# Row tiles 4 to 7 are loaded after ctx parts 12 to 14 have been quantised, instead of among parts 6 to 12

## The chip, the cores and the metric

The kernel runs on one core of a Trainium2 chip. The metric is device microseconds (us) for one execution. The kernel before was timed three times; the median counts. One further execution was profiled, and all rows below come from that one.

## The reference

x has 2 batches of 1024 rows of 2048 columns, ctx has 2 batches of 2048 by 2048. All data is float32.

```python
q1 = fake_quant(layernorm(x), x1_scale, x1_zp)     # clip(round(v/s + z), 0, 255), then (q - z)*s
q2 = fake_quant(ctx, x2_scale, x2_zp)
x  = x + q1 @ q2                                   # 1024x2048 by 2048x2048, per batch
qg, qu = quantised rows of layernorm(x)*inv_gate, layernorm(x)*inv_up
inter  = clip(silu(qg @ w_gate.T * scales) * (qu @ w_up.T * scales), -10, 10)
x  = x + (quantised rows of inter*inv_inter) @ w_down.T * scales
```

Only the first product, for the first batch, has to do with the change.

## The kernel before

**Tiles.** The 2048 rows of x are 16 row tiles of 128 rows (tile m, 1 MB each, `x_tile` in the trace). Tiles 0 to 7 are batch 0. ctx comes in 32 parts of 1 MB (part q, `ctx_stage`); four parts make one chunk of 512 columns, so parts 0 to 15 are batch 0. Stage one has 64 groups of 16 matmuls. Groups 0 to 15 multiply row tiles 0 to 3 with chunks 0 to 3 (group g takes tile g % 4 and chunk g // 4); groups 16 to 31 multiply tiles 4 to 7 with the same four chunks. Group 8 is thus the first to need parts 8 to 11, group 12 the first to need parts 12 to 15, group 16 the first to need tile 4.

**What happens to a ctx part.** A DMA of the ACT queue (L439) brings it into one of three staging buffers. DVE quantises it (L762) to eight bits, or ACT (L446) where q % 4 is 3; ACT (L455) or POOL (L698) casts it to fp16 for TensorE. ACT issues later parts between its casts: the load of part q waits until part q - 3 has been quantised. DVE also adds up the cast parts (`col_add`, L779 and L782) for a column sum, which TensorE multiplies by ones (L1048) after groups 6, 9, 11 and 14.

**What happens to a row tile.** SP issues its load (L259). DVE takes its statistics (L789), POOL makes the scale (L652 to L656), ACT quantises it (`x_i`, L462) and casts it (`x_q`, L470). For tiles 4 and up SP then issues a DMA transpose (`q1T`, L266). There is a single `x_q` buffer: the cast of tile m waits until the transpose of tile m - 1 has landed.

**What sets the order.** Each engine runs a list written out by hand, in step with the groups. On DVE, at group g, the column sums come first, then the quantisation of a part (part 12 at group 8, 13 at 9, 14 at 10), then row statistics (tile 4 at group 10, 5 at 11, 6 at 13, 7 at 14), and last the evacuation of group g (L808), which waits for its matmuls. On SP the list of loads 0 to 7 is followed by the transposes of tiles 4 to 6, the store of x2 tile 0 (L270), the transpose of tile 7, the stores of x2 tiles 1 to 3 and the loads of tiles 8 to 11. Tiles 4 to 7 go to space in SBUF of their own, so that their loads wait for no buffer: the wait on `c_quant` in front of each one only places them in time. `c_quant` counts the parts that DVE has quantised, and `plain(q)` is its count when part q is done.

Of the kernel before, what the change touches and what calls it, by code (L numbers as in the profile page):

```python
# [12 lines left out]
def build(nc, x, ctx_t, params, w_gu, sw_gu, w_dn, sw_dn, inv_gate, inv_up, inv_inter, out):  # L13
# [23 lines left out]
    with ExitStack() as stack:  # L37
# [5 lines left out]
        def sem(name):  # L43
            return stack.enter_context(nc.semaphore(name))
# [84 lines left out]
        c_quant, c_cast = sem("c_quant"), sem("c_cast")  # L129
# [91 lines left out]
        def plain(q):  # L221
            return q + 1 - (q + 1) // 4
# [21 lines left out]
        def _(sp):  # L244
            def load_x(m):
                if 4 <= m < 8:
                    sp.wait_ge(c_quant, plain((6, 8, 10, 12)[m - 4]))
                elif 8 <= m < 12:
                    sp.wait_ge(x2_stored[m % 8], 16)
                elif m == 13:  # L250
                    sp.wait_ge(c3_cast, QUADS // 4)
                elif m in (12, 14):
                    sp.wait_ge(c_quant, plain(30 if m == 12 else 29))
                elif m == 15:
                    sp.wait_ge(x2_stored[0], 32)
                if m == 0:
                    sp.dma_start(X[0][:, 0:D // 2], x_f[0:P, 0:D // 2]).then_inc(x_loaded[0], 16)
                    return
                sp.dma_start(X[m][:, :], x_f[m * P:(m + 1) * P, :]).then_inc(x_loaded[m % 8], 16)  # L259
# [56 lines left out]
            for m in range(8):  # L316
                load_x(m)
# [6 lines left out]
            for m in range(8, 12):  # L324
                load_x(m)
# [4 lines left out]
            for m in range(12, 15):  # L330
                load_x(m)
# [816 lines left out]
```

## Time and profile before

| what | value |
|---|---|
| median of 3 runs | 1054.46 us (1053.47 to 1055.18) |
| the profiled execution: its time, and its span | 1058.52 us, 1056.8 us |
| TensorE (PE) busy in the span | 939.6 us, 89% |
| VectorE (DVE), ScalarE (ACT), GpSimd (POOL) busy | 666.1, 360.4, 295.3 us |
| mean granted TensorE clock | 0.950 of full speed |
| loads of x on SP: count, size, median to landing | 15, 1024 KB, 9.4 us |
| loads of ctx on ACT: count, size, median to landing | 32, 1024 KB, 8.1 us |

The span is the time from the first to the last instruction; the profiled time holds 1.7 us more. A shift of one stage counts only if what follows starts earlier or later by it.

### The profile page before, as it was taken

The page shows a single profiled execution, that of the slowest core. Times are in us where ns is not written, and L with a number is a line of the kernel's source. Part 1 is how long each engine was busy: PE and PEld are TensorE (multiplying, and loading weights), DVE is VectorE, ACT ScalarE, POOL GpSimd, SP SyncE. Part 2 cuts the span into 40 slices and gives each one's busy share as a digit, 9 for nine tenths or more (in the row PEclk, how much of TensorE's full clock was granted, in tenths as well). Part 3 has the DMA queues.
Part 4 walks back from the last instruction along what each step waited for, and adds up shares of the span by engine and source line. Part 5 has one row for each costly group of instructions (what it writes and reads, how often), then busy time and mean ns, then how long its engine had stood idle before and what let it go on. Part 6 is the DMA issues. An engine that isn't in the chain of part 4 may idle for free.

```text
span 1056.8 us, 11253 instructions
## 1 busy us (share of the span) xinstructions
PE 939.6 (89%) x4192; PEld 416.0 (39%) x4192; DVE 666.1 (63%) x1006; ACT 360.4 (34%) x281; POOL 295.3 (28%) x256
## 2 busy tenths in 40 slices
PE   1689886799696778899999999999959989999998
PEld 1333332344242333344444444444424434444443
DVE  5469374657396777666777777777566694444443
ACT  4735456456445652222222333333226520000000
POOL 2226655364356021333333323223420000000000
PEclk9799988899897888899999999999989989999999
DMA  9665797976848803231333333333349630994112
GB/s 356 240 268 199 245 368 227 350 271 204 289 165 274 282 21 78 79 71 54 89 90 90 90 90 90 90 90 90 80 125 336 255 110 1 314 347 136 80 80 79
DMA packets 131686, 179.52 MB, mean 170 GB/s; under 512 B 111024, under 2 KB 111024, under 8 KB 113968
## 3 DMA queue, kind: packets, MB, share of 16 engines
q1 hardware_dynamic: 126848, 144.72, 43.8%
q10 hardware_dynamic: 4752, 34.08, 8.1%
q8 instruction: 33, 0.54, 0.2%
q0 software_dynamic: 32, 0.00, 0.1%
q14 instruction: 21, 0.17, 0.1%
HBM read 113.77 MB, written 37.75 MB: 143 GB/s over the span
## 4 chain that ended last, share of the span: by engine, by line
PE 58%; DVE 12%; issue 10%; DMA 8%; POOL 5%; ACT 5%; ACTq 0%; SPq 0%; DVEq 0%; POOLq 0%
PE ps L1099 36%; PE ps L1111 19%; DVE w_slots L849 5%; POOL x_tile L691 3%; PE ps L1079 3%; DMA ctx_stage<-in_ctx 2%; DVE small_operands L789 2%; DMA q1T<-x_q 2%; ACT x_i L462 1%; DMA w_raw<-in_w_gu 1%; DMA x_tile<-in_x 1%; DMA w_raw<-in_w_dn 1%; DVE ctx_u L762 1%; POOL ctx_slot L698 1%; DMA qT_odd<-q_f 1%
## 5 line engine op out<-in xcount | busy, mean ns | idle before, releaser
L1079 PE MATMUL ps<-ctx_slot,q1T 128*128 128x512 f16 x1024 | 237.2, 394 | 22.5 <-DMA q1T<-x_q 11.1
L1099 PE MATMUL ps<-w_slots,qT_even 128*128 128x512 f16 x1024 | 233.5, 391 | 21.1 <-issue 8.6
L1099 PE MATMUL ps<-w_slots,qT_odd 128*128 128x512 f16 x1024 | 231.9, 389 | 21.8 <-issue 19.7
L1111 PE MATMUL ps<-w_slots,qiT 128*128 128x512 f16 x1024 | 224.1, 382 | 4.1 <-DVE gate_and_up L891 4.1
L1079 PEld LDWEIGHTS ps<-ctx_slot,q1T 128*128 128x128 f16 x1024 | 102.7, 101 | 154.4 <-issue 16.8
L1099 PEld LDWEIGHTS ps<-w_slots,qT_even 128*128 128x128 f16 x1024 | 102.0, 100 | 151.8 <-issue 32.2
L1099 PEld LDWEIGHTS ps<-w_slots,qT_odd 128*128 128x128 f16 x1024 | 101.8, 100 | 151.2 <-issue 35.2
L1111 PEld LDWEIGHTS ps<-w_slots,qiT 128*128 128x128 f16 x1024 | 100.8, 99 | 127.3 <-DVE w_slots L849 4.6
L529 ACT ACTIVATE q_f<-q_i 128x2048 f16<-128x2048 int8 x32 | 61.1, 1910 | 195.0 <-DVE q_i L861 190.1
L920 DVE SCALAR_TENSOR_TENSOR down_tmp<-ps,small_operands,down_scales_b 128x512 f32<-128x512 f32 x64 | 48.0, 750 | 99.3 <-PE ps L1111 99.2
L870 DVE TENSOR_REDUCE small_operands<-x_and_xs 128x1 f32<-128x2048 f32 x19 | 43.4, 2284 | 105.9 <-POOL x_and_xs L672 102.3
L691 POOL TENSOR_TENSOR x_tile<-x_tile,col_bias 128x512 f32<-128x512 f32 x64 | 92.5, 1467 | 39.4 <-DVE x_tile L808 39.4
L808 DVE SCALAR_TENSOR_TENSOR x_tile<-ps,small_operands,x_tile 128x512 f32<-128x512 f32 x64 | 46.6, 734 | 57.1 <-PE ps L1079 56.9
L849 DVE SCALAR_TENSOR_TENSOR w_slots<-w_raw,small_operands,w_slots 128x1024 f16<-128x1024 f32 x48 | 68.7, 1430 | 13.9 <-ACT w_slots L507 10.4
L663 POOL TENSOR_SCALAR small_operands<-small_operands 128x1 f32<-128x1 f32 x16 | 4.0, 251 | 261.4 <-DVE small_operands L792 261.4
L672 POOL TENSOR_TENSOR x_and_xs<-h_bf,inv_gate_b 128x2048 f32<-128x2048 bf16 x16 | 65.5, 4092 | 39.2 <-ACT h_bf L517 39.2
L455 ACT ACTIVATE ctx_slot<-ctx_u 128x2048 f16<-128x2048 uint8 x24 | 45.5, 1905 | 74.4 <-DVE ctx_u L762 48.3
L507 ACT ACTIVATE w_slots<-w_raw,small_operands 128x1024 f16<-128x1024 f32 x48 | 52.4, 1139 | 30.2 <-DVE small_operands L832 17.4
L684 POOL TENSOR_TENSOR xs_up<-h_bf,inv_up_b 128x2048 f32<-128x2048 bf16 x13 | 53.2, 4096 | 0.0
L925 DVE SCALAR_TENSOR_TENSOR x_tile<-x_tile,small_operands,down_tmp 128x512 f32<-128x512 f32 x64 | 48.1, 752 | 2.3
L517 ACT ACTIVATE h_bf<-x_and_xs,small_operands 128x2048 bf16<-128x2048 f32 x15 | 31.4, 2093 | 53.0 <-POOL small_operands L666 53.0
L789 DVE BATCH_NORM_STATS2 small_operands<-x_and_xs 128x6 f32<-128x512 f32 x60 | 37.1, 681 | 8.7 <-DMA x_and_xs<-x_scratch 8.3
(91 smaller groups left out, 679.1 us busy)
## 6 DMA issues: line engine op xcount, KB each, us to landing
ctx_stage<-in_ctx ACTq DMA_DIRECT2D x32, 1024.0 KB, 8.1
x_scratch<-x_tile SPq DMA_DIRECT2D x16, 1024.0 KB, 5.0
w_raw<-in_w_gu SPq DMA_DIRECT2D x16, 1024.0 KB, 9.1
x_tile<-x_scratch SPq DMA_DIRECT2D x16, 1024.0 KB, 8.4
x_tile<-in_x SPq DMA_DIRECT2D x15, 1024.0 KB, 9.4
x_and_xs<-x_scratch SPq DMA_DIRECT2D x15, 1024.0 KB, 5.8
out_x<-x_tile SPq DMA_DIRECT2D x15, 1024.0 KB, 5.1
w_raw<-in_w_dn SPq DMA_DIRECT2D x8, 1024.0 KB, 9.2
```

Source lines behind the costliest of these rows:

```text
L507: nc.scalar.activation(hi[:, a * 2 * CW:(a + 1) * 2 * CW], raw[:, raw_unit(p, g), a * 2 * CW:(a + 1) * 2 * CW], ACT.Identity, bias=0.0, sc ...
L529: nc.scalar.activation(q16[:, :], q8[:, :], ACT.Copy).then_inc(q16_ready[which], 1)
L672: nc.gpsimd.tensor_tensor(bufA[:, :], hb[:, :], invg_b[:, :], ALU.mult).then_inc(xs_ready[0], 1)
L684: nc.gpsimd.tensor_tensor(dst[:, :], hb[:, :], invu_b[:, :], ALU.mult).then_inc(xs_ready[1], 1)
L691: nc.gpsimd.tensor_tensor(part, part, colb[:, j % 4, :], ALU.add).then_inc(adj_done, 1)
L789: ins = nc.vector.bn_stats(stats[:, 6 * c:6 * c + 6], src[:, c * CW:(c + 1) * CW])
L849: nc.vector.scalar_tensor_tensor(lo[:, cols], raw[:, raw_unit(p, g), cols], wsc[:, p:p + 1], hi[:, cols], ALU.mult, ALU.subtract).then_inc ...
L920: nc.vector.scalar_tensor_tensor(tmp[:, i % 2, :], ps[:, bank(S3 + i), :], si[:, t:t + 1], swd_b[:, c, :], ALU.mult, ALU.mult).then_inc(ev ...
L925: nc.vector.scalar_tensor_tensor(part, part, rterm[:, t:t + 1], tmp[:, i % 2, :], ALU.add, ALU.add).then_inc(res_done, 1)
L1079: last = nc.tensor.matmul(ps[:, bank(g), :], q1T[m][:, k, :], ctx_s[j % 4][:, k, :], start=(k == 0), stop=(k == KT - 1))
L1099: last = nc.tensor.matmul(ps[:, bank(S2 + i), :], qT[t % 2][:, which, k, :], wsl[:, unit(p, k // 4), hl, k % 4, :], start=(k == 0 and hl = ...
L1111: last = nc.tensor.matmul(ps[:, bank(S3 + i), :], qiT[t % 8][:, k, :], wsl[:, unit(4 + c, k // 4), hl, k % 4, :], start=(k == 0 and hl == ...
```

## The change

One tuple of wait values differs. Before, the loads of row tiles 4, 5, 6 and 7 wait until ctx parts 6, 8, 10 and 12 are quantised; after, until parts 12, 13, 14 and 14 are. Nothing is added or removed, and no other queue's list is touched.

```diff
             def load_x(m):
                 if 4 <= m < 8:
-                    sp.wait_ge(c_quant, plain((6, 8, 10, 12)[m - 4]))
+                    sp.wait_ge(c_quant, plain((12, 13, 14, 14)[m - 4]))
                 elif 8 <= m < 12:
                     sp.wait_ge(x2_stored[m % 8], 16)
```

## Rows read from the trace of the kernel before

**Rows 1.** Chain of work that ended last, 60 to 77 us: start us, us, what.
```profile
60.04 7.92 DMA ctx_stage<-in_ctx
...
67.98 1.36 DVE ctx_u L762
...
71.62 2.09 ACT ctx_u L446
...
73.78 2.66 POOL ctx_slot L698
```

**Rows 2.** Timeline of PE, 60 to 140 us: start, length, line, tiles, count, idle before.
```profile
67.89 6.21 PE L1079 MATMUL ps<-ctx_slot,q1T 128*128 128x512 f16 x28
76.49 6.18 PE L1079 MATMUL ps<-ctx_slot,q1T 128*128 128x512 f16 x20 [2.40 <-POOL ctx_slot L698]
...
91.92 1.04 PE L1048 MATMUL ps<-ctx_colacc,ones 128*128 128x512 f16 x4 [1.48 <-DVE ctx_colacc L782]
...
104.97 10.52 PE L1079 MATMUL ps<-ctx_slot,q1T 128*128 128x512 f16 x48
115.79 3.63 PE L1079 MATMUL ps<-ctx_slot,q1T 128*128 128x512 f16 x16 [0.30 <-DMA q1T<-x_q]
122.19 18.09 PE L1079 MATMUL ps<-ctx_slot,q1T 128*128 128x512 f16 x83 [2.77 <-DMA q1T<-x_q]
```

**Rows 3.** Windows: busy time of each engine, granted clock, DMA share, GB/s.
```profile
62.00:71.00 9.00, 9.00 (x44) 4.11 (x42) 6.37 (x7) 3.95 (x3) 0.00 (x0) 1.00 1.00 419
78.00:80.00 2.00, 2.00 (x7) 0.66 (x5) 1.95 (x3) 0.00 (x0) 2.00 (x2) 0.50 0.99 418
80.00:90.00 10.00, 10.00 (x47) 4.47 (x46) 9.15 (x10) 3.99 (x3) 3.31 (x2) 0.98 0.86 342
93.80:96.80 3.00, 3.00 (x16) 1.37 (x14) 2.79 (x5) 2.97 (x4) 2.49 (x6) 1.00 0.00 0
```

**Rows 4.** Load of tile 4, issued at 43.8; tile 5, at 60.0; tile 11, at 130.7.
```profile
x_tile<-in_x SPq DMA_DIRECT2D x1, 1024.0 KB, 8.2
x_tile<-in_x SPq DMA_DIRECT2D x1, 1024.0 KB, 7.6
x_tile<-in_x SPq DMA_DIRECT2D x1, 1024.0 KB, 19.4
```

**Rows 5.** Loads of parts 6 and 7, alone, issued at 34.4 and 34.8.
```profile
DMA to landing us min/median/max: 4.7/5.9/7.0
```

**Rows 6.** Timeline of DVE, 60 to 88 us: column sums, quantisations, an evacuation.
```profile
64.44 1.22 DVE L782 TENSOR_TENSOR ctx_colacc<-ctx_colacc,ctx_slot 128x2048 f16<-128x2048 f16 x1
67.98 1.35 DVE L762 TENSOR_SCALAR ctx_u<-ctx_stage,small_operands 128x2048 uint8<-128x2048 f32 x1 [2.32 <-DMA ctx_stage<-in_ctx]
...
71.54 0.75 DVE L808 SCALAR_TENSOR_TENSOR x_tile<-ps,small_operands,x_tile 128x512 f32<-128x512 f32 x1 [0.43 <-PE ps L1079]
...
73.34 1.34 DVE L762 TENSOR_SCALAR ctx_u<-ctx_stage,small_operands 128x2048 uint8<-128x2048 f32 x1
...
79.89 2.28 DVE L762 TENSOR_SCALAR ctx_u<-ctx_stage,small_operands 128x2048 uint8<-128x2048 f32 x1
...
86.11 1.34 DVE L762 TENSOR_SCALAR ctx_u<-ctx_stage,small_operands 128x2048 uint8<-128x2048 f32 x1
```

**Rows 7.** Timeline of ACT, 90 to 127 us, the casts of tiles 4 and 5.
```profile
94.80 1.91 ACT L470 ACTIVATE x_q<-x_i 128x2048 f16<-128x2048 int8 x1
...
101.26 1.91 ACT L470 ACTIVATE x_q<-x_i 128x2048 f16<-128x2048 int8 x1 [1.90 <-DMA q1T<-x_q]
```

**Rows 8.** Transposes of tile 4, issued at 96.8; tile 8, at 146.0; tile 9, at 159.3.
```profile
q1T<-x_q SPq DMA_TRANSPOSE x1, 4.4
q1T<-x_q SPq DMA_TRANSPOSE x1, 8.0
q1T<-x_q SPq DMA_TRANSPOSE x1, 9.2
```

**Rows 9.** Timeline of DVE, 124 to 137 us: the statistics of tile 8.
```profile
133.83 2.47 DVE L789 BATCH_NORM_STATS2 small_operands<-x_tile 128x6 f32<-128x512 f32 x4 [2.52 <-DMA x_tile<-in_x]
```

## The prediction, made before the changed kernel was run

> **What bounds the kernel now.** TensorE is busy for 89% of the span, but that average says nothing about 60 to 125 us, where the four loads stand. I read that stretch in four views. First the chain of work [rows 1]: at 60.04 it is on the DMA of ctx part 10, then passes through DVE's quantisation of part 10, ACT's quantisation of part 11 and POOL's cast of part 11 to the matmuls of group 8. The reader is to see that TensorE stood still there for 2.40 us, and that the 20 matmuls behind the gap took 6.18 us where 28 had taken 6.21 just before [rows 2]: the granted clock was 0.50, the 1.2 GHz level, right behind the gap [rows 3]. Part 10 was late because it shared the DMA engines with tile 5: issued at 60.03 and 60.04, they landed 7.6 and 7.92 us later [rows 1, 4], where part 6, alone, took 4.7 [rows 5].
>
> Then the end of the stretch. Groups 18 and 19 wait for a transpose, 0.30 and 2.77 us [rows 2]. These transposes are a chain of their own: with one `x_q` buffer, each cast of a row tile waits for the transpose before it (1.90 us for that of tile 5), from 94.80, the cast of tile 4, to the landing for group 19 at 122.19 [rows 2, 7]. Whatever is won before 94.80 must pass through this chain to count. So the question is not what part 10 gains, but when the transpose of tile 4 lands: before, 96.83 + 4.4 = 101.2 [rows 8].
>
> **Part 10 and group 8: a gain of 4.1 us on TensorE, for the moment.** Without tile 5 beside them, I price parts 10 and 11 as parts 6 and 7 alone: 60.04 + 4.7 = 64.7 and, issued 0.4 us behind like part 7, 60.44 + 7.0 = 67.4 [rows 5]. DVE is free for part 10 when its column sum ends at 64.44 + 1.22 = 65.66 and no longer waits until 67.98 [rows 6], 2.3 us earlier. All that follows moves with it: ACT's quantisation of part 11 to 69.3 (the part is there at 67.4), POOL's cast to 71.5 and its end, with the same 2.66 us, to 74.1. TensorE wants it at 67.89 + 6.21 = 74.1 [rows 1, 2]. So the gap of 2.40 goes, to 0.1 at most, and with it the half-speed matmuls: 20 at the pace of the 28 are 4.4 us, 6.18 - 4.4 = 1.7. Together 4.1 us. The other end is zero, if part 10 lands as late as before.
>
> **Tile 4 moves from 43.8 to 74.7: nothing for what it leaves.** Its 8.2 us [rows 4], shared with part 9, ended at 52.0, eight us ahead of the load on the chain of work [rows 1]. Where it goes it counts: its wait, part 12, ends at 73.34 + 1.34 = 74.7 as before, since the evacuation of group 7, waiting for TensorE, sets DVE there, not a load [rows 6].
>
> **Tiles 5 to 7.** DVE now runs ahead. Group 8 ends at 75.0 (the last four matmuls at full pace), its evacuation begins at 75.1 and takes 0.7, a column sum 1.2 (as the 1.22 at 64.44), then part 13 runs from 77.0 to 78.3 (79.3 with the 2.28 it took before), where tile 5 is issued. TensorE ends group 9 at 78.5 (3.5 us a group: 48 matmuls in 10.52 [rows 2]) and its own column product of 1.04 at 79.5; two column sums of DVE behind it lead to part 14 at 82.0. Part 14 is issued at 74.7 beside tile 4, as part 9 beside tile 4 before, or part 10 beside tile 5: 7.6 to 8.2 us, so 82.3 to 82.9 [rows 4]. It ends at 83.7 to 84.3 instead of 86.11 + 1.34 = 87.45 [rows 6], and there SP issues tiles 6 and 7, which before had been issued by 74.7, the end of part 12. What is queued behind these waits on SP is only the transpose of tile 4, which comes later anyway. Who waits for the loads is DVE: the statistics of tile 4 at 84 find it landed; those of tile 5 come 2.7 (a row tile's statistics), 0.7 and 1.2 us later, at 88.6, and find it if it lands by then. So the advance of 4.1 shrinks to about 3.4 by the wait for part 14, and TensorE, which waits behind group 11 for DVE's column sum (1.48 us before [rows 2]), starts group 12 about 3.4 us early.
>
> **When tile 7 lands.** From 74.7 on both queues are full: SP has tiles 4 to 7, ACT parts 14 to 17, eight MB. The first pair lands at 82.3 to 82.9, as above. A pair is 2.1 MB; at the 419 GB/s of 62 to 71 us [rows 3] each further pair takes 5.0 us, so tile 5 lands at 87.3 to 87.9, tile 6 at 92.3 to 92.9, and tile 7 at 97.3 to 97.9. Before, nothing moved any more at 93.8 to 96.8 [rows 3], and the transpose of tile 4 met empty queues.
>
> **Where the gain is given back.** The cast of tile 4 is ready 3.4 us early, at 91.4, and its transpose is issued at 93.5. But the load of tile 7 stands before it in SP's queue. The trace has this case once: tile 11 was issued at 130.7 and landed 19.4 us later, at 150.1 [rows 4]; the transpose of tile 8, issued at 146.0 behind it, landed at 154.0 [rows 8], 3.9 us after tile 11, not 4.4 after its own issue. By this the transpose of tile 4 lands at 97.3 + 3.9 = 101.2 to 97.9 + 3.9 = 101.8, against 101.2 before: 0 to 0.6 us later. The other ends: not held at all, 93.5 + 4.4 = 97.9, 3.3 us earlier; or the 9.2 us of tile 9's transpose, which ran beside ctx parts on the other queue [rows 8]: 102.7, 1.5 us later. I take no change, as the row of tile 8 is the same queue in the same order.
>
> The casts and transposes of tiles 5 to 7 then run at their old times, since all loads have landed by then, and group 19 starts at 122.2 again. TensorE's 3.4 us turn into longer waits before groups 17 and 18. If the clock drops behind those, up to 1.7 us as at 76.49, the late evacuation of group 19 has cover: DVE waits 2.52 us for tile 8 at 133.83 [rows 9]. Without that cover it would cost those 1.7.
>
> **The sum.** 4.1 gained at group 8, 0.7 lost to part 14, 3.4 lost to the transpose of tile 4: 0. The profiled execution stays at a span of 1056.8 and a time of 1058.52; that one lies 4.06 above the median of the runs. For the median I forecast 1054.5.
>
> **The rivals.** Faster: the transpose isn't held by tile 7, or tile 7 lands by 94, and the 3.3 us go through to the end: 1054.5 - 3.3 = 1051.2. For it speaks that TensorE and DVE really are ahead until 101, and that later stages follow group 19; against it the row of tile 8.
>
> Slower: the eight MB come more slowly than I priced, and the transpose is late by more than it was early. At the 342 GB/s of 80 to 90 us [rows 3], 8.4 MB take 24.5 us; begun at 77.3 (2.6 after the issue, the 7.6 of tile 5 less 5.0 for its pair) they end at 101.8, the transpose lands at 105.7, and the end is 4.5 us later: 1059.0. It decides by more than 2.1 us from a landing of tile 7 at 99.4. Against it: the 342 holds the emptying of the queues near 90, and with both full the trace has 418 to 419. The Trainium skill ("DMA: Bandwidth & Descriptors", section Bandwidth) puts HBM's share of a core at about 358 GB/s for loads to SBUF, with 425 measured for 16 MB when the pair's other core is idle. By the 358 the eight loads would take an estimated 23.4 us and end at 100.7, 3.4 us late and near this rival; the trace, with 419 while one core runs, agrees with the other figure.
>
> No effect at group 8: part 10 is no faster without tile 5, because something else was in its way. Then tiles 6 and 7 are issued at 87.5 as DVE keeps its old times; the pairs still follow each other from 82.9 by 5.0, tile 7 lands at 97.9, and the transpose of tile 4 at 101.8: 0.6 us later, 1055.1.
>
> **How the numbers follow.** About 0.2%, 2.1 us, is what a measurement can tell from no change. The forecast has a chance of 0.52 and the case without effect at group 8 0.10, both within it: same 0.62. The faster rival has 0.22, since one row alone shows a transpose behind a load; the slower one 0.16. The likeliest case by itself spans 1053.0 to 1056.0 (the landing of the first pair, 9.2 instead of 8.0 for the transpose). For 8 in 10 the range reaches down to the faster rival with 1051.0, and up into the slower one to 1057.0.
>
> **What the profile after would show.** Part 10 landing near 64.7 and no gap before the last matmuls of group 8; clock 1.00 at 78 to 80; group 12 some 3 us early; tile 7 landing near 97 and the transpose of tile 4 not before 101; group 19 again near 122 behind waits longer than before. I am wrong if tile 4's transpose lands near 98 (faster), or if tile 7 lands after 99.4, or DVE stands at the statistics of tile 5 for several us (slower).

## The result, and the profile after

The changed kernel took 1059.24 us (median of 20 runs, 1056.26 to 1063.15) against 1055.88 us for the kernel before (20 runs, 1051.09 to 1060.37): a ratio of 1.0031 with a 95% interval of 1.0017 to 1.0045. It is slower, by 3.3 us with 1.8 to 4.8 as bounds. The profiled execution of the changed kernel took 1059.55 us with a span of 1057.8, only 1.0 us more than the profiled one of before; but that one lay 2.6 us above the median of its kernel, this one 0.3. A difference of 3 us can't be read off two executions. What can be read is what happens in them. Ratios here and below leave out slow runs, those more than 1.5% above the fastest of the same kernel; medians in us hold all runs.

TensorE after, timeline of 40 to 260 us, the rows that answer to [rows 2]:

```profile
67.74 10.52 PE L1079 MATMUL ps<-ctx_slot,q1T 128*128 128x512 f16 x48
78.66 1.04 PE L1048 MATMUL ps<-ctx_colacc,ones 128*128 128x512 f16 x4 [0.40 <-DVE ctx_colacc L782]
...
90.08 1.88 PE L1048 MATMUL ps<-ctx_colacc,ones 128*128 128x512 f16 x4 [3.47 <-DVE ctx_colacc L782]
91.75 11.41 PE L1079 MATMUL ps<-ctx_slot,q1T 128*128 128x512 f16 x48
...
115.42 3.63 PE L1079 MATMUL ps<-ctx_slot,q1T 128*128 128x512 f16 x16 [0.82 <-DMA q1T<-x_q]
121.81 24.35 PE L1079 MATMUL ps<-ctx_slot,q1T 128*128 128x512 f16 x112 [2.77 <-DMA q1T<-x_q]
```

The 2.40 us gap in group 8 is gone, and so are the half-speed matmuls: groups 7 to 9, 48 matmuls, run through in 10.52. TensorE is 3.8 us ahead when the column product behind group 9 begins (78.66 against 82.50). Behind group 11 it loses most of that again, waiting 3.47 us for DVE where before it was 1.48. Behind this longer wait the clock falls as well: at 90 to 92 us the granted clock is 0.53, almost all of it at the 1.2 GHz level, the column product takes 1.88 us instead of 1.04, and the 48 matmuls behind it 11.41 instead of 10.52. Group 12 starts at 91.75, only 1.0 us earlier than in TensorE's timeline of before:

```profile
92.79 10.52 PE L1079 MATMUL ps<-ctx_slot,q1T 128*128 128x512 f16 x48
```

DVE after, timeline of 56 to 140 us, the rows that answer to [rows 6]:

```profile
65.43 1.34 DVE L762 TENSOR_SCALAR ctx_u<-ctx_stage,small_operands 128x2048 uint8<-128x2048 f32 x1
...
72.06 2.12 DVE L782 TENSOR_TENSOR ctx_colacc<-ctx_colacc,ctx_slot 128x2048 f16<-128x2048 f16 x1
74.11 2.28 DVE L762 TENSOR_SCALAR ctx_u<-ctx_stage,small_operands 128x2048 uint8<-128x2048 f32 x1
...
78.53 2.29 DVE L762 TENSOR_SCALAR ctx_u<-ctx_stage,small_operands 128x2048 uint8<-128x2048 f32 x1
...
84.28 1.34 DVE L762 TENSOR_SCALAR ctx_u<-ctx_stage,small_operands 128x2048 uint8<-128x2048 f32 x1
...
90.87 2.47 DVE L789 BATCH_NORM_STATS2 small_operands<-x_tile 128x6 f32<-128x512 f32 x4 [0.85 <-DMA x_tile<-in_x]
```

Part 10 no longer waits (65.43 against 67.98). But the column sum and part 12 behind it take 2.12 and 2.28 us instead of 1.22 and 1.34, so part 12, which sets off the loads, ends at 76.4 instead of 74.7. The statistics of tile 5, the last row, now wait 0.85 us for its load. GpSimd's rows say what ran beside DVE: its cast of part 11 (L698) and its adjustments (L691), which apply the column sums' correction (`col_bias`) to row tiles. First the adjustments before, then cast and adjustments after:

```profile
76.40 6.90 POOL L691 TENSOR_TENSOR x_tile<-x_tile,col_bias 128x512 f32<-128x512 f32 x4
```

```profile
71.22 1.90 POOL L698 TENSOR_SCALAR ctx_slot<-ctx_u 128x2048 f16<-128x2048 uint8 x1 [21.29 <-ACT ctx_u L446]
73.08 8.86 POOL L691 TENSOR_TENSOR x_tile<-x_tile,col_bias 128x512 f32<-128x512 f32 x4
```

The cast, to 73.1, now stands beside the column sum from 72.06. The adjustments begin 3.3 us earlier and now stand beside part 12, and both engines are slower for it.

DMA issues after: loads of tiles 4 to 7, issued at 76.4, 80.8, 85.6 and 86.0, then the transpose of tile 4, issued at 95.2; the last number is the time to landing in us (compare [rows 4, 8]):

```profile
x_tile<-in_x SPq DMA_DIRECT2D x1, 1024.0 KB, 7.1
x_tile<-in_x SPq DMA_DIRECT2D x1, 1024.0 KB, 10.0
x_tile<-in_x SPq DMA_DIRECT2D x1, 1024.0 KB, 10.2
x_tile<-in_x SPq DMA_DIRECT2D x1, 1024.0 KB, 14.0
q1T<-x_q SPq DMA_TRANSPOSE x1, 7.4
```

Tile 7 lands at 86.0 + 14.0 = 100.0, and the transpose, issued 1.7 us earlier than before, lands at 95.15 + 7.4 = 102.6 instead of 101.2. ACT shows it as the wait of the next cast, 4.36 us where it was 1.90 [rows 7]:

```profile
102.64 1.91 ACT L470 ACTIVATE x_q<-x_i 128x2048 f16<-128x2048 int8 x1 [4.36 <-DMA q1T<-x_q]
```

And the queues, windows of after (last two columns: DMA share and GB/s): at 93.8 to 96.8, empty before [rows 3], they are full.

```profile
76.40:100.00 23.60, 19.73 (x84) 8.27 (x83) 21.65 (x26) 15.06 (x10) 15.36 (x17) 0.93 0.98 364
93.80:96.80 3.00, 3.00 (x16) 1.34 (x15) 2.08 (x3) 2.51 (x4) 2.61 (x6) 1.00 1.03 429
```

Yet group 19 starts at 121.81, not later than the 122.19 of before. In before's execution the transpose of tile 5 took 6.0 us (issued 103.29), in after's 4.3, and that paid the 1.4 back. Was 6.0 the rule for the kernel before, or chance? On this hung two theories: **A**, the loss is complete by group 19, through the transpose of tile 4 held up behind tile 7's load; **B**, nothing is lost by group 19, and the loss arises in later stages. A third, **C**, came up with the first experiments: the queue is innocent, and DVE, slowed by GpSimd, makes everything it feeds late.

### The profile page after: what moved, and what is told of

It is laid out like the page before. It is cut to its first block, busy times and chain, and to the rows that moved or that the text cites. A ratio compares the mean times of both kernels' runs of the same rounds, so it can differ in the third digit from the quotient of the medians.

```text
span 1057.8 us, 11253 instructions
## 1 busy us (share of the span) xinstructions
PE 936.1 (88%) x4192; PEld 414.8 (39%) x4192; DVE 668.9 (63%) x1006; ACT 360.5 (34%) x281; POOL 296.6 (28%) x256
## 3 DMA queue, kind: packets, MB, share of 16 engines
q1 hardware_dynamic: 126848, 144.72, 43.7%
## 4 chain that ended last, share of the span: by engine, by line
PE 58%; DVE 12%; issue 10%; DMA 9%; POOL 5%; ACT 5%; SPq 0%; ACTq 0%; DVEq 0%; POOLq 0%
PE ps L1099 36%; PE ps L1111 18%; DVE w_slots L849 5%; PE ps L1079 3%; POOL x_tile L691 3%; DMA q1T<-x_q 3%; DMA x_tile<-in_x 2%; DMA ctx_stage<-in_ctx 2%; DVE small_operands L789 1%; DMA w_raw<-in_w_gu 1%; DMA w_raw<-in_w_dn 1%; ACT x_i L462 1%; DMA qT_odd<-q_f 1%; ACT w_slots L507 1%; DVE ctx_u L762 1%
## 5 line engine op out<-in xcount | busy, mean ns | idle before, releaser
L1079 PEld LDWEIGHTS ps<-ctx_slot,q1T 128*128 128x128 f16 x1024 | 102.9, 101 | 152.8 <-issue 17.8
L1099 PEld LDWEIGHTS ps<-w_slots,qT_even 128*128 128x128 f16 x1024 | 101.4, 100 | 154.9 <-issue 32.3
L1099 PEld LDWEIGHTS ps<-w_slots,qT_odd 128*128 128x128 f16 x1024 | 101.1, 99 | 147.8 <-issue 31.4
L691 POOL TENSOR_TENSOR x_tile<-x_tile,col_bias 128x512 f32<-128x512 f32 x64 | 94.6, 1499 | 40.8 <-DVE x_tile L808 40.8
L517 ACT ACTIVATE h_bf<-x_and_xs,small_operands 128x2048 bf16<-128x2048 f32 x15 | 31.4, 2093 | 52.7 <-POOL small_operands L666 52.7
```

The lines of the kernel that those rows point to most:

```text
L691: nc.gpsimd.tensor_tensor(part, part, colb[:, j % 4, :], ALU.add).then_inc(adj_done, 1)
L1079: last = nc.tensor.matmul(ps[:, bank(g), :], q1T[m][:, k, :], ctx_s[j % 4][:, k, :], start=(k == 0), stop=(k == KT - 1))
L1099: last = nc.tensor.matmul(ps[:, bank(S2 + i), :], qT[t % 2][:, which, k, :], wsl[:, unit(p, k // 4), hl, k % 4, :], start=(k == 0 and hl = ...
```

## The experiments

**Both kernels ended after group 19.** A stretch of 140 us shows 2 us more plainly than 1056 do. The cut is the same in each (DVE's, ACT's, GpSimd's and TensorE's lists end, SP writes out row tiles 0 to 3):

```diff
-            for g in range(G1):
+            for g in range(20):
...
+            sp.wait_ge(evac_done, 20)
+            for m in range(4):
+                sp.dma_start(out_f[m * P:(m + 1) * P, :], X[m][:, :]).then_inc(out_stored[m], 16)
...
+            return
```

> The kernel before, ended after group 19: no later ctx part, row tile, weight or product is loaded or computed, and row tiles 0 to 3 are written out as they stand, so the output is not the reference's. It is the yardstick for cut20_after, with the same cut. Theory A (the loss is complete by group 19: the transpose of tile 4 comes late behind tile 7's load, and the chain of casts and transposes carries it): this one is 1.4 to 3.4 us faster than cut20_after. Theory B (nothing is lost by group 19, 121.81 against 122.19 us in the two profiles; the loss arises in later stages): the two agree within 0.6 us. By either its time is near 140 us.

> The changed kernel, ended after group 19 in the same way. Theory A: 1.4 to 3.4 us slower than cut20_before. Theory B: within 0.6 us of it.

Measured: 139.14 us (137.94 to 140.19) before, 141.30 (140.37 to 143.12) after; as ratios to the full kernel before 0.1313 (0.1307 to 0.1320) and 0.1337 (0.1332 to 0.1343), which is 2.5 us apart. The loss is there by group 19: theory A, as far as the place goes, and B falls. The trace of the cut kernel before also answers the question about before. First its load of tile 7, issued at 76.06, and its transpose of tile 4, issued at 95.50; then the same two of the cut changed kernel, issued at 85.03 and 94.00:

```profile
x_tile<-in_x SPq DMA_DIRECT2D x1, 1024.0 KB, 7.1
...
q1T<-x_q SPq DMA_TRANSPOSE x1, 4.3
```

```profile
x_tile<-in_x SPq DMA_DIRECT2D x1, 1024.0 KB, 12.6
...
q1T<-x_q SPq DMA_TRANSPOSE x1, 6.1
```

Executions differ by nearly 4 us in when they reach this stretch, so the table counts from the start of group 3 (53.20 us before, 53.05 after, and 50.7 to 54.5 elsewhere; it is the row of 64 matmuls behind a wait of 2.04). Each entry is an issue plus its time to landing, less that start.

| kernel | tile 7 lands | transpose of tile 4 issued, lands | transpose of tile 7 lands |
|---|---|---|---|
| before, full | 30.2 | 43.6, 48.0 | 68.9 |
| before, cut | 30.2 | 42.5, 46.8 | 67.6 |
| changed, full | 46.9 | 42.1, 49.5 | 68.7 |
| changed, cut | 45.6 | 41.9, 48.0 | 68.7 |
| tile 7 behind the transpose, cut | 49.7 | 41.9, 46.3 | 67.2 |
| tile 4 put back, cut | 45.3 | 41.9, 47.6 | 67.1 |
| all four early, cut | 7.2 | 41.9, 46.3 | 65.8 |
| before with the hold, cut | 31.4 | 49.7, 54.3 | 73.6 |

The execution of before that was profiled in full was a late one in this stretch, by 1.3 us at the last transpose. In each of the six cut traces of the table the kernel ends 17.8 to 18.1 us behind the landing of tile 7's transpose, so this landing sets the time of a cut kernel. Against the cut kernel before, the transpose of tile 4 is 1.2 us late in the cut changed one and that of tile 7 1.1 us.

The chain doesn't hand a delay on one for one, though: it has room at tile 6. In the cut kernel before the transpose of tile 5 landed at 106.25, but ACT's quantisation of tile 6 had waited for GpSimd's scale, and its cast began 1.6 us after that landing:

```profile
105.71 2.10 ACT L463 ACTIVATE x_i<-x_tile,small_operands 128x2048 int8<-128x2048 f32 x1 [3.82 <-POOL small_operands L660]
107.84 1.91 ACT L471 ACTIVATE x_q<-x_i 128x2048 f16<-128x2048 int8 x1
```

In the cut changed kernel the 1.2 us would have fitted into this room; but its transpose of tile 5 took 5.7 us where that of the cut kernel before took 4.3. In the full changed kernel the transpose of tile 5 took 4.3 us, and the 2.7 us by which that of tile 4 was late (49.5 against 46.8) went beyond the room by 1.1. Why a transpose of tile 5 takes 4.3 us in one execution and 5.7 to 6.0 in another, before the change as behind it, stays open.

**Tile 7's load behind the transpose of tile 4, nothing else moved.** First in the cut form, then full.

```diff
-            for m in range(8):
+            for m in range(7):
                 load_x(m)
-            for m in range(4, 7):
+            transpose_x(4)
+            load_x(7)
+            for m in range(5, 7):
                 transpose_x(m)
```

> The changed kernel, ended after group 19, with the load of tile 7 put behind the transpose of tile 4 in SP's list; nothing else moves. With the same cut the kernel before took 139.14 us and the changed one 141.30. Theory A (the transpose of tile 4 is late because tile 7's load stands before it in SP's queue): it now follows tile 6, lands some 2 to 3 us earlier, and the time falls to 138.5 to 139.5. Theory C (the queue is innocent; GpSimd's adjustments, now 3.3 us earlier, slow VectorE's column sums and quantisations of parts 12 and 13, 2.12, 2.28 and 2.29 us instead of 1.22, 1.34 and 1.34, and all that DVE feeds is late): no load order helps, 141 to 142.

> The full changed kernel with the load of tile 7 put behind the transpose of tile 4 in SP's list; output as the reference's. Its cut form took 139.34 us where the changed kernel's took 141.30 and before's 139.14. Theory A (what is late at group 19 is late at the end): the loss is gone, 0.998 to 1.001 of before against 1.0031 for the change. Theory B (the late loads cost most of it in later stages, by way of what they shift): 1.002 to 1.004, as the change.

Measured: 139.34 us cut (137.50 to 140.72), where the change has 141.30 and before 139.14, as ratios 0.1308 (0.1303 to 0.1314), 0.1337 and 0.1313; 0.9992 full (0.9975 to 1.0009; 1056.83 us against 1056.91). The loss is gone with one load moved past one transpose, while DVE is slowed as in the change: theory A, against C. (The move takes the load's megabyte out of the transpose's way together with its place in the queue; no run separates the two.) In the cut trace the transpose, issued at 93.61, and the load, issued at 95.42 behind it:

```profile
q1T<-x_q SPq DMA_TRANSPOSE x1, 4.3
...
x_tile<-in_x SPq DMA_DIRECT2D x1, 1024.0 KB, 5.9
```

The transpose takes its 4.3 us again although tile 6 landed only at 93.7 in this trace; the load behind it still lands at 101.4, in time for its statistics.

**The transpose of tile 4 held back in the kernel before, no load moved.** This is the other direction: a late transpose alone.

```diff
                 sp.wait_ge(xq_ready, m + 1)
+                if m == 4:
+                    sp.wait_ge(evac_done, 14)
```

> The same hold in the kernel before ended after group 19 (139.14 us without the hold). Theory A and the rest alike expect the chain to carry it to group 19: 143 to 145 us. If it is 139 to 140, the chain isn't what sets group 19, and theory A falls.

> The kernel before, with the transpose of tile 4 alone held back until group 13 is evacuated: issued near 102.7 instead of 96.8 us, no load moved. Theory A: the chain of casts and transposes hands the delay on to group 19 and to the end, 4 to 6 us more, 1.004 to 1.006 of before. Theory B: a late transpose is covered by waits in later stages; no more than 1 us, 0.999 to 1.001.

Measured: 145.15 us cut (142.15 to 148.01), as a ratio 0.1352 (0.1345 to 0.1360), 4.1 us more than without; 1.0058 full (1.0041 to 1.0076), 6.1 us more (the medians, 1064.20 and 1056.91, are 7.3 apart). The transpose of tile 4 landed 5.7 us later after group 3 in the full trace (53.7 against 48.0), 7.5 in the cut one, and that of tile 7 4.0 and some 6 us later. Most of what is late at the transpose of tile 4 is late at the end. In the cut trace the rest went into the room at tile 6; in the full one the transpose of tile 5 took 4.3 us, where the profiled execution of before had 6.0. TensorE of the full kernel with the hold waits for each transpose in turn, at groups 17, 18 and 19:

```profile
112.18 3.63 PE L1081 MATMUL ps<-ctx_slot,q1T 128*128 128x512 f16 x16 [1.82 <-DMA q1T<-x_q]
118.58 5.31 PE L1081 MATMUL ps<-ctx_slot,q1T 128*128 128x512 f16 x16 [2.78 <-DMA q1T<-x_q]
124.97 5.36 PE L1081 MATMUL ps<-ctx_slot,q1T 128*128 128x512 f16 x24 [1.07 <-DMA q1T<-x_q]
```

**Tile 4 put back behind part 6.** `plain((6, 13, 14, 14)[m - 4])`, full and cut.

> The change with tile 4 put back behind part 6, tiles 5 to 7 late as in the change: one MB less in the burst from 76 us. Theory A: tile 7 lands some 2.5 us earlier than the 100.0 of the changed kernel and the transpose of tile 4 at 100 to 101 instead of 102.6: 0.998 to 1.001 of before. Theory B: tiles 5 to 7 are as late as in the changed kernel, and the time is the changed kernel's: 1.002 to 1.004.

> The change with tile 4 put back behind part 6, ended after group 19: in the full kernel's trace tile 7 landed 49.1 us after group 3 began, and the transpose of tile 4 took 5.4 us. Theory A: in between, 139.5 to 141 us (before 139.14, the change 141.30). If DVE's slowing alone made the loss (2.28 us for part 12 in this kernel too): 141 to 142.

Measured: 1.0007 full (0.9984 to 1.0029; 1057.26 us), 139.81 us cut (137.57 to 141.38), as a ratio 0.1307 (0.1301 to 0.1313). By the ratio the cut kernel isn't in between, as A had it, but free of the loss (0.1337 for the change, 0.1313 before), with DVE's part 12 at 2.29 us all the same; the full interval overlaps the change's and settles nothing alone. With one MB less tile 7 lands at 45.3 in the table instead of 45.6, and in the full trace at 45.0 instead of 46.9 (the 49.1 of the second expectation is a misreading): less than the 2.5 us expected, since tiles 6 and 7 are issued when part 14 is done, at 32.6 after group 3 in both. The transpose of tile 4 is only 0.4 us earlier than in the cut changed kernel; the transpose of tile 5, with 4.6 us instead of 5.7, gives the rest in this trace.

**All four tiles behind part 6.** `plain((6, 6, 6, 6)[m - 4])`, full and cut.

> Row tiles 4 to 7 all wait for ctx part 6 and so fill the time from 44 to 58 us, when the trace of before shows empty queues from 52 to 60. Both theories expect parts 10 and 11 to land near 64.7 and 67.2 as in the changed kernel, and no gap in group 8. Theory A: no load stands before the transpose of tile 4, which lands near 97 (4 us earlier than before), and the end follows: 0.996 of before, 1051 to 1053 us. Theory B: an earlier group 19 is worth nothing by itself; later stages set the end, 0.999 to 1.003.

> Tiles 4 to 7 all loaded behind part 6, ended after group 19. Theory A: no load stands before the transpose of tile 4; by the full kernel's trace group 19 starts 1.8 to 3.1 us earlier after the start of group 3 than before: 136 to 137.5 us against 139.14 for before. Theory C: DVE is slowed as in the changed kernel (2.12, 2.28, 2.29 us in the full kernel's trace), so no better than the changed kernel's 141.3 or, at best, before's 139.1.

Measured: 0.9993 full (0.9974 to 1.0012; 1056.47 us against 1056.46), 138.46 us cut (137.04 to 140.02), as a ratio 0.1301 (0.1295 to 0.1306). No load stands before the transposes, the last one lands at 65.8, 1.8 us earlier than in the cut kernel before. Cut it is faster than before by 1.3 us (0.1313), which theory C doesn't allow; full the forecast of 0.996 is missed, and the interval, which reaches 2.7 us faster, neither shows this gain nor excludes it. The reason that the traces show for so little is that the transpose of tile 4 is issued at 41.9 to 42.1 after group 3 in every kernel of the table in which part 10 comes early, whatever the order of the loads: not 3.4 us earlier than before, but 0.4 to 1.7.

**GpSimd's adjustments kept back until group 10**, in the changed kernel and in the one with all four tiles early, both cut:

```diff
-        while n < G1 and (g == G1 or n < g and n - first < 2 and bias_step[chunk_of[n]] < g):
+        while n < G1 and (g == G1 or n < g and g >= 10 and n - first < 2 and bias_step[chunk_of[n]] < g):
```

> The changed kernel, ended after group 19, with GpSimd's adjustments kept back until group 10 (before: from group 8), so that none runs beside DVE's quantisations of parts 12 and 13. If GpSimd is what slows DVE, column sum and quantisations take 1.22 and 1.34 us again, part 12 ends 1.7 us sooner and so do the loads of tiles 4 to 7 begin. Theory A: tile 7 and the transpose behind it land 1.7 us sooner, 139.5 to 140 us. Theory C: all that DVE lost comes back, 138.5 to 139.5. If GpSimd isn't what slows DVE: 141.3.

> The same with GpSimd's adjustments kept back until group 10: neither a load before the transpose nor a slowed DVE. Both theories expect the least time of all cut kernels; A and C together some 1.5 to 2.5 us less than without the adjustments kept back, 134 to 136 us. If the adjustments kept back are missed later (the store of x2 tile 0 waits for the first thirteen), nothing is won over the other.

Measured: 144.07 us (140.61 to 146.71) and 140.74 (139.98 to 142.88), as ratios 0.1334 (0.1328 to 0.1340) and 0.1333 (0.1326 to 0.1339). By the ratios the first is no better than the change (0.1337), and the second slower than without (0.1301); the gains that A and C expected are missed. DVE of the first, the column sum and part 12, then the column sum and part 13:

```profile
71.61 2.12 DVE L787 TENSOR_TENSOR ctx_colacc<-ctx_colacc,ctx_slot 128x2048 f16<-128x2048 f16 x1
73.66 1.33 DVE L767 TENSOR_SCALAR ctx_u<-ctx_stage,small_operands 128x2048 uint8<-128x2048 f32 x1
...
75.57 1.21 DVE L787 TENSOR_TENSOR ctx_colacc<-ctx_colacc,ctx_slot 128x2048 f16<-128x2048 f16 x1
76.70 1.34 DVE L767 TENSOR_SCALAR ctx_u<-ctx_stage,small_operands 128x2048 uint8<-128x2048 f32 x1
```

So GpSimd is what slows DVE: without adjustments beside them parts 12 and 13 take 1.33 and 1.34 us again (the first sum runs beside GpSimd's cast of part 11, and stays at 2.12). In the changed kernel the loads didn't end sooner: tiles 6 and 7 still waited for part 14, issued 32.9 and 33.3 after group 3, and tile 7 landed at 46.1.

With all four tiles early, where no load is in the way, the transpose of tile 4 is issued 39.4 us after group 3 instead of 41.9 and lands at 43.7 instead of 46.3. These 2.6 us are what the adjustments beside DVE cost the cast of tile 4: without them it is 3.1 us ahead of the cut kernel before (42.5). The kernel as a whole gains nothing by it, because adjustments kept back are missed later. GpSimd's scale for tile 6 comes behind them, so that its transpose is issued at 55.5 (55.1 without). And the store of x2 tile 0 comes late and is issued 0.4 us ahead of the transpose of tile 7, which takes 6.5 us (4.3 without) and lands at 68.9 instead of 65.8. So what C says of DVE is right about the gain that doesn't arrive, and A is right about the loss.

## Why the prediction was wrong

**Part 10 and group 8: right, for the execution that was read.** Part 10 landed at 64.70 (forecast 64.7), the gap and the half-speed matmuls went; TensorE was 3.8 us ahead after group 9 for the 4.1 forecast. But the 4.1 us were not there in every execution of before. TensorE behind the same gap, first in the full kernel with the hold, which does the same work up to there, then in the cut kernel before:

```profile
75.29 4.49 PE L1081 MATMUL ps<-ctx_slot,q1T 128*128 128x512 f16 x20 [2.40 <-POOL ctx_slot L700]
```

```profile
75.00 4.49 PE L1085 MATMUL ps<-ctx_slot,q1T 128*128 128x512 f16 x20 [1.15 <-POOL ctx_slot L702]
```

The 20 matmuls took 4.49 us in both, not 6.18. Counted from group 3, the column product behind group 9 begins at 29.3 us in the profiled execution of before, at 27.6 and 26.4 in these two, and at 25.6 after the change: the change wins 3.7, 2.0 or 0.8 us there.

**Tiles 4 to 7: the first wrong step.** The wait of tile 4's load, part 12, was to end "at 73.34 + 1.34 = 74.7 as before": it ended at 76.4. I moved DVE's and GpSimd's work on each engine by its own, and didn't see that GpSimd's cast of part 11 and its adjustments, freed by part 11 coming earlier, would land on DVE's column sum and part 12. The cast cost the sum 0.90 us, the adjustments part 12 0.94, and at part 13 0.41 for the sum and 0.95 over the 1.34 that I counted with. The 2.28 of part 13 in [rows 6], beside an adjustment too, was the sign; I had it as the other end only. The "0.7 lost to part 14" became 2.8 (a lead of 3.8 after group 9, 1.0 at group 12): 2.0 by the longer wait for DVE and 0.8 by the lower clock behind it. The "3.4 us early" of the cast of tile 4 became 1.7: 93.12 against 94.80, and its transpose was issued at 95.15, not 93.5.

**When tile 7 lands: the term that was too small.** Forecast 97.3 to 97.9, measured 100.0. The first pair landed at 83.5 instead of 82.3 to 82.9, by the late part 12; the three pairs behind it took 16.5 us to tile 7 (83.52 to 100.0), 5.5 each and not 5.0. Its loads also had no 419 GB/s throughout: 364 as the mean over 76.4 to 100.

**Where the gain is given back: right in kind, wrong in size.** The transpose waited for tile 7 and landed 2.6 us after it, at 102.6. That is the mechanism of the forecast, and the Trainium skill has it too ("DMA: Bandwidth & Descriptors", section "Queues, rings and completion order"): on each DMA engine a ring's descriptors are consumed in order, and a transpose from SP shares its ring with SP's loads. The trace agrees, with 7.4 us for the transpose behind the load and 4.3 in front of it. But I took "no change" from a range of 0 to 0.6 us later, and it was 1.4 later than in before's profiled execution and 2.7 later, after group 3, than in the cut kernel before. This is the step that failed: the load of tile 7 was priced to land 2.1 to 2.7 us too early, so the hold on the transpose was counted as just using up the gain, where it cost more than there was.

**The yardstick.** I compared with 101.2 as if every execution of before had it. The cut kernel before has the transpose landing 1.2 us earlier after group 3, and its chain of four ends 1.3 us earlier. "The casts and transposes of tiles 5 to 7 then run at their old times" took over a 6.0 us transpose of tile 5 that didn't return (4.3 in the cut kernel). Between the two cut traces the loss is 1.2 us for the transpose of tile 4 and 1.1 for that of tile 7, less than the 2.5 us between the kernels: the profiled run of the cut kernel before was the longest of its five (140.19 us), that of the changed one the shortest of its six (140.37). The forecast of 1054.5 was also built on a median of three runs; that of twenty is 1055.88, which makes 1.4 of the 4.7 us by which it missed.

**The rivals.** The slower one came true by its place and its threshold (tile 7 after 99.4; measured 100.0), by a late start and slower pairs together rather than by 342 GB/s; it had 0.16. That its 1059.0 is so near the measured 1059.24 is luck: it had the transpose land at 105.7 (measured 102.6), and its median of before was 1.4 us too low. The 358 GB/s of the Trainium skill ("DMA: Bandwidth & Descriptors", section "Bandwidth") was not the limit: the trace has 429 at 93.8 to 96.8, near the 425 that the same section gives for a core whose neighbour is idle. The faster rival had no ground: TensorE's lead never reached the cast of tile 4 whole.

What stays open: why the full kernels differ by 3.3 us (1.8 to 4.8) where the cut ones differ by 2.5. The intervals overlap; a further loss in later stages is neither shown nor excluded.

## What to carry to other kernels

A transfer that is moved away from a stall on a queue lands in front of something else on that queue: look up what the queue issues next, and whether a chain of single-buffered steps starts there. Here the load of tile 7 cost nothing where it ran among other loads, and some 2.5 us in front of the first of four transposes that hand most of a delay on; put behind that transpose it costs nothing again. When engines that share work are moved, lay their new times side by side, since a pair of instructions that now coincides can take back the gain, here 2.6 us; and before trusting a difference of 1 us, profile a second execution or cut the stretch out and time it.

## What was not expected of the hardware

DVE and GpSimd slow each other by no fixed share. Beside an adjustment, DVE's quantisation took 2.28 us instead of 1.34 (+0.94) and a column sum 1.63 instead of 1.22 (+0.41); beside GpSimd's cast a column sum took 2.12 (+0.90); and each of the four adjustments took 2.23 to 2.25 us, where the quickest of before took 1.25. With the adjustments moved away the quantisation was back at 1.34 and the sum at 1.21. The Trainium skill ("SBUF — State Buffer", section "SBUF: two separate sides") says that the two engines share a pair of ports as an exclusive lock, held for a whole instruction, where DVE's instruction is in a two-port mode or has two inputs in SBUF. Alternating whole instructions fit these rows roughly: a sum that takes 1.22 us alone ended 1.06 us behind the end of the cast, another 1.09 behind that of an adjustment. But no run here separates a lock from another kind of sharing.
